# Vision tower on one core: the first convolution stage runs two halves ahead instead of one, and the image patches of a unit come in two transfers instead of six

## What is computed

```python
x = _conv2d(x, conv1_w, conv1_b)               # 3 -> 64 channels
residual = x
x = jax.nn.gelu(_group_norm(x, gn1_g, gn1_b), approximate=False)
x = _conv2d(x, rconv1_w, rconv1_b)             # 64 -> 64
x = jax.nn.gelu(_group_norm(x, gn2_g, gn2_b), approximate=False)
x = _conv2d(x, rconv2_w, rconv2_b)
x = _conv2d(residual + x, proj_w, proj_b, stride=P, pad=0)
```

## Time and profile before

| what | value |
|---|---|
| runs | 2082.00, 2076.85, 2090.18 us, median 2082.0 |
| profiled execution: its own time | 2084.01 us |
| its span, first to last instruction | 2082.2 us |
| mean granted TensorE clock | 0.90 of full |
| busy: PE, DVE, ACT, POOL | 1634.7, 1224.6, 947.6, 907.6 us |

### The profile page before, as it was taken

How to read it: one execution, slowest core, us unless ns; L and a number is a source line. 1 busy time by engine, 2 the same in 40 slices (tenths; PEclk the granted TensorE clock), 3 DMA queues, 4 the chain that set the end, 5 groups by cost and what they waited for, 6 DMA issues and landing times. The chain is left out here.

```text
span 2082.2 us, 45356 instructions
## 1 busy us (share of the span) xinstructions
PE 1634.7 (79%) x13560; PEld 1054.4 (51%) x13560; DVE 1224.6 (59%) x4296; ACT 947.6 (46%) x2114; POOL 907.6 (44%) x2183
## 2 busy tenths in 40 slices
PE   7899956777877687777877777687778775798899
PEld 2344423334655455545654555365545554665556
DVE  8876756775656556555665556565565555148240
ACT  3466535554444444444445444444444442032442
POOL 2000036665555555545555555455555552024220
PEclk9999989998989889989998999899888997897789
DMA  5522242223333333333333333333333337620000
GB/s 148 175 83 81 82 172 73 73 73 99 101 92 81 96 92 102 82 91 96 101 84 93 97 94 93 79 104 95 92 86 98 101 90 196 164 50 1 1 1 12
DMA packets 120494, 188.61 MB, mean 91 GB/s; under 512 B 22575, under 2 KB 90350, under 8 KB 120198
## 3 DMA queue, kind: packets, MB, share of 16 engines
q1 hardware_dynamic: 120326, 186.41, 33.5%
HBM read 103.06 MB, written 19.69 MB: 59 GB/s over the span
## 5 line engine op out<-in xcount | busy, mean ns | idle before, releaser
L499 PE MATMUL rc<-sb_acts,sb_rwd 128*64 128x512 f16 x1764 | 651.0, 446 | 336.2 <-DMA sb_acts<-sb_hst 336.1
L500 PE MATMUL rc<-sb_acts,sb_rwd 128*64 128x512 f16 x1764 | 652.2, 446 | 0.0
L414 ACT ACTIVATE sb_f32q<-c,sb_gsh,sb_gsc 128x128 f32<-128x128 f32 x788 | 297.0, 458 | 573.0 <-POOL sb_gsh L368 573.0
L499 PEld LDWEIGHTS rc<-sb_acts,sb_rwd 128*64 128x64 f16 x1764 | 193.1, 124 | 466.5 <-DMA sb_acts<-sb_hst 381.3
L357 POOL TENSOR_TENSOR sb_tmp<-sb_mst 128x4 f32<-128x4 f32 (+1 forms) x296 | 84.6, 286 | 756.3 <-DVE sb_mst L782 756.2
L362 POOL TENSOR_TENSOR sb_tmp<-sb_tmp,sb_half_neg 128x4 f32<-128x4 f32 (+1 forms) x296 | 386.7, 1306 | 23.2
L423 ACT ACTIVATE sb_g2f<-rc,sb_gsh,sb_gsc 128x128 f32<-128x128 f32 x784 | 296.8, 469 | 165.7 <-POOL sb_gsh L368 154.3
L499 PE MATMUL rc<-sb_acts,sb_rwl 128*64 128x512 f16 x1176 | 367.2, 394 | 3.8 <-issue 3.4
L500 PE MATMUL rc<-sb_acts,sb_rwl 128*64 128x512 f16 x1176 | 366.7, 394 | 0.0
L553 PE MATMUL pj<-sb_wall,sb_arena 128*64 128x384 f16 x1792 | 317.7, 357 | 18.8 <-DMA sb_wall<-w_lo 9.9
L782 DVE TENSOR_REDUCE sb_mst<-st 128x8 f32<-128x16 f32 (+1 forms) x296 | 52.6, 178 | 463.0 <-PE st L541 463.0
(11 more groups left out here) (161 smaller groups left out, 2573.8 us busy)
## 6 DMA issues: line engine op xcount, KB each, us to landing
sb_acts<-sb_hst SPq DMA_DIRECT2D x788, 78.8 KB, 2.1
sb_wall<-w_lo SPq DMA_DIRECT2D x56, 528.0 KB, 3.9
sb_im<-x_planes SPq DMA_DIRECT2D x300, 60.7 KB
sb_wall<-w_lo SPq DMA_DIRECT2D x28, 480.0 KB, 3.7
sb_im<-x_planes SPq DMA_DIRECT2D x300, 30.3 KB
sb_f32q<-in_proj SPq DMA_DIRECT2D x12, 576.0 KB, 4.5
sb_arena<-in_proj SPq DMA_DIRECT2D x12, 576.0 KB, 4.8
w_lo<-sb_arena SPq DMA_DIRECT2D x1, 6144.0 KB, 17.0
```

The lines of the kernel that those rows point to most:

```text
L414: ins = nc.scalar.activation(g1f[:, q * Q + m, :], c1[q][:, m * HALF:(m + 1) * HALF], ACT.Gelu, bias=gsh[q][:, m:m + 1], scale=gsc[q][:, m ...
L499: nc.tensor.matmul(out[0:CH, :], w_odd, x_odd, start=(n == 0), stop=(n == 14))
L500: yield nc.tensor.matmul(out[CH:128, :], w_even, x_even, start=(n == 0), stop=(n == 14))
```

## The change

The first stage is moved one half step further ahead of the middle convolution. In slot `k` TensorE now does the means of half `k+3` and conv1 of half `k+4` (before `k+2` and `k+3`), DVE reads the means of half `k+3` and splits half `k+2` (before `k+2` and `k+1`), and POOL and ACT are shifted alike. One more half is done in the prologue on each engine. Since conv1 of half `2u+4` is now in the even slot `2u`, the wait for the image rows of unit `u+2` moves there too. SP's order in a unit is now `double(2u + 2)`, `load_im(u + 2)`, `double(2u + 3)`.

`x_planes` gets six more planes (a second copy of the high ones), so that a unit can be loaded in two transfers of 54 rows; before there were three of 24 rows and three of 12 rows. The rows are the same in number (108) and length (1294 f16 values). The rows of `w1s` stand in another order, and are placed by 12 small transfers at the start (before 2); the zero planes are written by 6 transfers (before 3).

```diff
-    scr = nc.dram_tensor("x_planes", (12, PLANE), F16)
+    scr = nc.dram_tensor("x_planes", (18, PLANE), F16)
...
-            sp.dma_start(w1s[0:KA, :], w1hl[0:KA, 0, :]).then_inc(s_w1s, 16)
-            sp.dma_start(w1s[KA:KC, :], w1hl[KA:KC, 1, :]).then_inc(s_w1s, 16)
+            for at in range(0, KC, 18):
+                sp.dma_start(w1s[at:at + 12, :], w1hl[at:at + 12, 0, :]).then_inc(s_w1s, 16)
+                sp.dma_start(w1s[at + 12:at + 18, :], w1hl[at + 12:at + 18, 1, :]).then_inc(s_w1s, 16)
...
-            for h in range(2):
-                sp.dma_start(bass.AP(tensor=scr, offset=h * 6 * PLANE, ap=[[7 * PAD, ROWS], [PLANE, 6], [1, 7 * PAD]]),
+            for k, h in enumerate((0, 1, 0)):
+                sp.dma_start(bass.AP(tensor=scr, offset=k * 6 * PLANE, ap=[[7 * PAD, ROWS], [PLANE, 6], [1, 7 * PAD]]),
...
             def load_im(u, p):
-                for kx in range(3):
-                    sp.dma_start(im[p][24 * kx:24 * kx + 24, 0:RUN],
-                                 bass.AP(tensor=scr, offset=u * (U * PAD) + kx,
-                                         ap=[[PLANE, 12], [WD, 2], [1, RUN]])).then_inc(s_im[p], 16)
-                    sp.dma_start(im[p][KA + 12 * kx:KA + 12 * kx + 12, 0:RUN],
-                                 bass.AP(tensor=scr, offset=u * (U * PAD) + kx,
-                                         ap=[[PLANE, 6], [WD, 2], [1, RUN]])).then_inc(s_im[p], 16)
+                for up in range(2):
+                    sp.dma_start(im[p][54 * up:54 * up + 54, 0:RUN],
+                                 bass.AP(tensor=scr, offset=u * (U * PAD) + up * WD,
+                                         ap=[[1, 3], [PLANE, 18], [1, RUN]])).then_inc(s_im[p], 16)
...
                         sp.wait_ge(s_c1, 2 * u + 3)
+                        double(2 * u + 2, 1 - p, 0)
                         load_im(u + 2, p)
-                        double(2 * u + 1, p, 1)
-                        double(2 * u + 2, 1 - p, 0)
+                        double(2 * u + 3, 1 - p, 1)
...
                 woven(1)
-                means(0, N1[q], 2 * u + q + 2, u - (q == 0) if k2 else 0)
+                means(0, N1[1 - q], 2 * u + q + 3, u - (q == 0) if k2 else 0)
                 woven(3)
-                if q == 1:
-                    pe.wait_ge(s_im[p], 96 * (pairs_done + 2))
-                pe.wait_ge(s_g1, 2 * u + q + 2)
-                conv1(1 - q, 1 - p if q == 0 else p)
+                if q == 0:
+                    pe.wait_ge(s_im[p], 32 * (pairs_done + 2))
+                pe.wait_ge(s_g1, 2 * u + q + 3)
+                conv1(q, p)
...
-                    dve.wait_ge(s_c1, k + 4)
-                    channel_stats(0, N1[q], c1[q], 0)
-                    moments(0, N1[q], 7 * (k + 2) + 4)
+                    dve.wait_ge(s_c1, k + 5)
+                    channel_stats(0, N1[1 - q], c1[1 - q], 0)
+                    moments(0, N1[1 - q], 7 * (k + 3) + 4)
...
-                    read_means(0, N1[q], k + 2)
-                    if q == 0:
-                        split1(k + 1, 1, p, (pair_at + p) if n2 else None)
-                    else:
-                        split1(k + 1, 0, 1 - p, pair_at + 1)
+                    read_means(0, N1[1 - q], k + 3)
+                    split1(k + 2, q, 1 - p, pair_at + 1)
```

More of the change, by code:

```diff
@@ L38 @@
 PLANE = (NPAT + 2 * U + 1) * PAD
-KA, KC = 72, 108
+KC = 108
 WS = 64.0
@@ L246, in _ @@
             for n, k in ((NPAT, U), (NPAT + U, U), (NPAT + 2 * U, 1)):
-                sp.dma_start(bass.AP(tensor=scr, offset=n * PAD, ap=[[PLANE, 12], [1, k * PAD]]),
-                             zt[:, 0:k * PAD]).then_inc(s_scr, 16)
+                for at, planes in ((0, 12), (12, 6)):
+                    sp.dma_start(bass.AP(tensor=scr, offset=at * PLANE + n * PAD, ap=[[PLANE, planes], [1, k * PAD]]),
+                                 zt[0:planes, 0:k * PAD]).then_inc(s_scr, 16)
             def load_im(u, p):
-                for kx in range(3):
-                    sp.dma_start(im[p][24 * kx:24 * kx + 24, 0:RUN],
-                                 bass.AP(tensor=scr, offset=u * (U * PAD) + kx,
-                                         ap=[[PLANE, 12], [WD, 2], [1, RUN]])).then_inc(s_im[p], 16)
-                    sp.dma_start(im[p][KA + 12 * kx:KA + 12 * kx + 12, 0:RUN],
-                                 bass.AP(tensor=scr, offset=u * (U * PAD) + kx,
-                                         ap=[[PLANE, 6], [WD, 2], [1, RUN]])).then_inc(s_im[p], 16)
+                for up in range(2):
+                    sp.dma_start(im[p][54 * up:54 * up + 54, 0:RUN],
+                                 bass.AP(tensor=scr, offset=u * (U * PAD) + up * WD,
+                                         ap=[[1, 3], [PLANE, 18], [1, RUN]])).then_inc(s_im[p], 16)
             with sp.Fori(3, FU // 2 - 1) as i:
@@ L260, in _ @@
                     fold_io(i, p, False)
-            sp.wait_ge(s_scr, 16 * 8)
+            sp.wait_ge(s_scr, 16 * 12)
             load_im(0, 0)
@@ L302, in _ @@
             double(0, 0, 0)
+            double(1, 0, 1)
             over_groups(sp, group)
@@ L334, in _ @@
             sp.wait_ge(s_emb, 32 * GROUPS + 32)
-            sp.wait_ge(s_dup[0][0], 64 * (UNITS // 2 + 1))
+            for q in range(2):
+                sp.wait_ge(s_dup[0][q], 64 * (UNITS // 2 + 1))
             sp.wait_ge(s_wr, 32)
@@ L372, in pair @@
                     u = u0 + p
-                    norm(0, 0, 2 * u + 2)
+                    norm(0, 1, 2 * u + 3)
                     if not (first and p == 0):
                         norm(1, N2[1 - p], u - 1)
-                    norm(0, 1, 2 * u + 3)
+                    norm(0, 0, 2 * u + 4)
             pool.wait_ge(s_padz, 3)
@@ L380, in _ @@
             norm(0, 1, 1)
+            norm(0, 0, 2)
             over_groups(pool, lambda g, b, first: over_units(pool, g, pair, first))
@@ L438, in pair @@
                         for q in range(2):
-                            gelu1(2 * u + 1 + q, 1 - q, not (first and p == 0 and q == 0))
+                            gelu1(2 * u + 2 + q, q)
                             if first and 2 * p + q < 3:
@@ L455, in _ @@
             gelu1(0, 0, False)
+            gelu1(1, 1, False)
             group(0, 0, True)
@@ L629, in _ @@
             pe.sem_inc(s_pj, 1)
-            pe.wait_ge(s_w1s, 32)
+            pe.wait_ge(s_w1s, 192)
             pe.wait_ge(s_rowz, 4)
-            pe.wait_ge(s_im[0], 96)
+            pe.wait_ge(s_im[0], 32)
             pe.wait_ge(s_tev, 3 * FU)
@@ L638, in _ @@
             means(0, 1, 1, 0)
-            pe.wait_ge(s_im[1], 96)
+            pe.wait_ge(s_im[1], 32)
             pe.wait_ge(s_g1, 1)
             conv1(0, 1)
+            means(0, 0, 2, 0)
+            pe.wait_ge(s_g1, 2)
+            conv1(1, 1)
             over_groups(pe, group)
-            means(1, N2[1], UNITS - 1, 2 * UNITS + 2)
+            means(1, N2[1], UNITS - 1, 2 * UNITS + 3)
             for c in range(NCH):
@@ L753, in _ @@
             dve.wait_ge(s_padz, 3)
-            dve.wait_ge(s_scr, 16 * 8)
+            dve.wait_ge(s_scr, 16 * 12)
             v.sem_inc(s_rd[0], 1)
@@ L862, in _ @@
             split1(0, 0, 0, None)
+            dve.wait_ge(s_c1, 4)
+            channel_stats(0, 0, c1[0], 0)
+            moments(0, 0, 7 * 2 + 4)
+            read_means(0, 0, 2)
+            split1(1, 1, 0, None)
             group(0, 0, True)
@@ L879, in _ @@
             dve.wait_ge(s_pj, GROUPS)
-            dve.wait_ge(s_sp1, K + 1)
+            dve.wait_ge(s_sp1, K + 2)
             dve.wait_ge(s_sp2, K + 2)
@@ L1537, in layout @@
                 par, up = dy % 2, dy // 2
-                rows = [kx * 24 + (6 * k + 2 * c + par) * 2 + up for k in range(2)] + [KA + kx * 12 + (2 * c + par) * 2 + up]
+                rows = [up * 54 + kx * 18 + 6 * k + 2 * c + par for k in range(3)]
                 for half in range(2):
```

2 lines of the change are left out of this document (1 added, 1 removed).

## The result

The changed kernel takes **2743.3 us** (median of 4 runs, 2739.8 to 2753.1), against 2080.4 us before on the same chip: ratio 1.318, 95% interval 1.313 to 1.324. It is 663 us slower. The forecast was 2685, range 2385 to 2850.

The account below looks back on a forecast made before the run. It took the chain to the doubled high part, with image loads ahead in SP's queue, to bound the kernel. Profiled 2084 + 589 (97 unit steps) + 6 (98th) + 8 (prologue) = 2687, median 2 lower: 2685 us, range 2385 to 2850.

Parts of the forecast that it names:

- The doubled part is not waited for any more: Before the middle convolution (L499) TensorE idled 336.2 us for the doubled high part; made one half earlier, this wait goes.
- A new wait for the image rows: In front of conv1 (L534) TensorE waits some 8 us once a unit, the load being issued behind double(2u+2).
- R: Start of DVE's read of the means in the even slot; TensorE was to go on 9.2 us later.
- 18 rows one after another in three lines: In the image load's data: rows go in sequence on three lines, 2.2 us a load, 4.4 for both.
- The second rival: In the image load's data: rows move side by side, TensorE goes on 3.1 us earlier; 2381 us, 17%.
- The length of a unit: From one unit to the next: 21.0 us with projection, 20.3 without; 97 steps take 2019 against 1430, +589.
- the 5 to 6 that I named as a sign: In the profile after, the image load lands 5 to 6 us behind its first issue.
- the second norm's chain: From conv1 over the second norm's means, POOL's norm and the statistics to DVE's next read; unit 21.0 us with projection.
- TensorE's chain: From TensorE's release through even and odd slots to DVE's next read; unit 20.7 us, 1.7 of it low clock.
- Prologue and 98th unit: In the prologue +8 us for added transfers ahead of a weight load; the last unit's wait +6.
- Mean clock near 0.9: A sign for the profile after: TensorE's mean clock near 0.9.
- The first rival: Image rows are there in time; the ring over POOL's second norm binds, 12.0 us a unit; 1823 us, 4%.

Follow-up runs that it names:

- shift_alone: The changed kernel with the six old image transfers at the new place instead of the two new ones; 2788.1 us, ratio 1.340.
- load_first: The changed kernel with load_im(u + 2) issued ahead of double(2u + 2), not behind it; 2353.2 us, ratio 1.131.
- unit_ahead: The changed kernel with load_im(u + 3) in the same queue place, load_im(2) in the prologue, and no conv1 wait at the unit's head; 1878.7 us, ratio 0.904.
- the cheap half of a change: The kernel before with only the image loads changed to two transfers a unit at the old place, no shift; 1957.9 us, ratio 0.942.
- the other half, made to work: The changed kernel with the six old image transfers, loaded one unit further ahead; 1867.8 us, ratio 0.899.

## Why the prediction was right

- **The doubled part is not waited for any more.** Right: 336.2 us to 2.0. shift_alone, with 2.0 as well, shows that the shift does this by itself.
- **A new wait for the image rows, once a unit, behind the doubling.** Right, and shown from both sides: one place earlier 390 us go, one unit ahead 865. Release at R + 9.44 in the turn shown, forecast R + 9.2.
- **18 rows one after another in three lines.** Right: the data of two loads takes 4 to 4.5 us (1217.5 to 1222), forecast 4.4, at 24 to 25 GB/s a line. The second rival (side by side, 2381) is out by the stretches of the kernel after. With the planes outermost the change would still be at 2566: more lines shorten it by 1.8 us a unit, not by the 3.1 of that rival.
- **The length of a unit.** Mechanism right, size short by 63 us: 20.84 us in the first 14 steps, where I had 20.3, and 21.57 over the other 83, where 20.9 was the mean of my terms. The term that was sized too small is the stretch from R to the release. The turn shown is one of the shortest there. The same rows of 96 turns (for one with projection: release 1588.09, means 1590.27, R 1599.71, load 1602.87, release 1609.48) give 9.82 us on average, 9.35 to 10.72, where I had 9.2, and 97 x 0.62 = 60 us. Of the 0.62, 0.2 lie ahead of the load's first issue (R + 3.2 for R + 3.0) and 0.4 between it and the release (6.6 for 6.2, and more than the 5 to 6 that I named as a sign). Why the landing is that much later was not taken apart. The other terms cancel: in the 25 turns without projection conv1 to the means took 1.70 for 1.8, the norm 3.33 for 3.2, from there to R 5.34 for 5.45; in the 71 with projection 2.18 for 2.5, 3.23 for 3.2 and 5.78 for 5.45. That the second norm's chain ends last also holds in the main: in 53 of those 71 VectorE does not wait for the means of R, in 18 it does, and there TensorE's chain is the longer one. The clock is at 0.50 for 3.9 us after TensorE goes on at 1222.32, where I had priced 3.4.
- **Prologue and 98th unit.** I had +14. The span less the 97 steps gives +6.4, so 8 us of the error of the unit are made up here by luck. Of SyncE's queue in the weight fold one row speaks to it:

```profile
88.87 12.88 SPq L249 DMA_DIRECT2D x_planes<-sb_arena  x6
```

  The three added zero transfers cost 12.88 less 6.25, 6.6 us of issues; the rest of the term can't be told from the place where the first unit's load now stands.
- **Mean clock near 0.9.** Wrong: 0.791. I had priced the 3.4 us after a stop and forgotten that the clock is low in the stop too. The low clock in the stop costs no time, since TensorE does nothing then.
- **The first rival (1823).** Its ring is real: 12.2 us between second norms once the load is early, and 1853 to 1879 us for four kernels. Its condition was the issue of the load over 9 us earlier; load_first, one slot earlier, did not reach it, unit_ahead did.

## To carry to other kernels

When work is moved a slot earlier, list what each of its inputs stands behind in its queue, down to the wait of the instruction ahead: a load behind a transfer that needs the same slot's result turns free time into 9 us a turn. If the queue has a gap only there, load for one turn further ahead; here that cost two small transfers and was worth 865 us. And try the cheap half of a change alone first: here it was better than the whole (1958 against 2743, and 1853 with the planes outermost), and the other half, made to work, added nothing.

## What the hardware showed that I had not expected

- A doubling behind a load that still runs on three lines lands after up to 5.6 us, against 3.5 in the kernel before (medians 2.6 and 2.1). With the planes outermost it is 3.9 and 2.1 again. So a transfer with few lines delayed its neighbour here, and not only its reader.
- More lines give less than in proportion: 4.4 us for 273 KB in three lines, and with the 18 planes outermost still the greater part of three rows of 1 us (98, 85 and 96 GB/s add up to 279 KB), at a share of 0.25 to 0.40. Against the 0.19 to 0.20 and 72 to 75 GB/s of the three lines, the share grows more than the rate. The second load of the pair is issued 0.9 us behind the first; how much of the loss is that was not tried.
- The granted clock in a stop does not fall at a fixed moment. Two stops of load_first: TensorE stops at 1202.0 and goes on at 1207.62, and stops again at 1219.93 and goes on at 1225.41. In the first the clock is still 1.00 (2.4 GHz) from 1202 to 1203 and 0.50 (1.2 GHz) from 1204 on. In the second it is 1.00 up to 1224.

```profile
1203.00:1204.00 1.00, 0.00 (x0) 0.00 (x0) 0.56 (x3) 0.36 (x1) 0.92 (x2) 0.86 0.64 163
1204.00:1205.00 1.00, 0.00 (x0) 0.00 (x0) 0.32 (x1) 0.00 (x0) 0.78 (x3) 0.50 0.65 166
...
1223.00:1224.00 1.00, 0.00 (x0) 0.00 (x0) 0.00 (x0) 1.00 (x4) 0.00 (x0) 1.00 0.51 134
1224.00:1225.00 1.00, 0.00 (x0) 0.00 (x0) 0.00 (x0) 0.39 (x2) 0.00 (x0) 0.60 0.13 47
```

  After these stops TensorE works at 0.50 until about 1210.6 and until 1231.0: 2.9 us after the first, 5.6 after the second, and 3.9 in the turn shown of the kernel after. So a stop of some microseconds is paid for twice: once by itself, and once by the microseconds at half the clock that follow it.
